# Attention and a two-expert part on one core: the attention's loop over pairs of batches written out batch by batch

## Chip, cores and metric

The kernel runs on one core of a Trainium2 chip. The metric is the device time of one execution in microseconds (us), lower is better; before the change three runs gave 1580.22, 1586.92 and 1582.1 us, median 1582.1.

## The reference

For x of 8 batches x 512 positions x 512 channels, in 32-bit floats:

```
xn  = (x - mean) / sqrt(var + 1e-5)                     # per position
qkv = xn @ Wqkv.T + b_qkv                               # 16 heads of 32
p   = softmax(q k^T / sqrt(32) + slope[h] * (k - 511), causal)
s   = (p v) @ Wout.T + b_out
e   = argmax(softmax(xn @ w_router.T)); w = its weight  # one of 2 experts per position
h   = xn @ w_fc[e].T;   a = (h if h >= 0 else h/2)^2    # 2048 wide
g   = silu(w * (a @ w_proj[e].T))
out = x + s * g
```

## The kernel before, in words

There are two blocks, one after the other, with a barrier between them. `attention_block` computes s for all positions and the routing table (which expert, its weight, the position's rank). `ffn_block` then runs 17 slots of 256 positions each, every slot with one expert's weights; it reads s back by gathered rows and writes the output by scattered rows. Its instructions are all written out, slot by slot (`slots`, a Python loop).

In `attention_block` every engine (TensorE, ScalarE, VectorE, GpSimd and the DMA queue of SyncE) has a function `iteration(b, odd)` that issues its share of "batch b". An iteration has 16 steps, one per head. In each step TensorE transposes the four causal strips of the normalised weights of one head (10 transposes of 128x128, `ptrans`, line 439, 160 in a batch), runs one or two jobs of the list `JOBS` (projections q, k, v, the output projection "o", the transposes of xn "x", the router's "logits" and "rank", and the weighted sum "ctx"), and computes the scores of a head four steps ahead (`scores`, line 418). VectorE masks scores and takes their minimum (line 791), forms reciprocals (line 802), and has the layer norm's statistics of the next batch in steps 0 and 1 (lines 683, 684), its application in steps 2 to 5 (line 690), and in step 13 `place`, a chain of small operations on 128x4 elements (lines 741 to 757), each of which waits for the one before through the semaphore `dve_link` (`link`). ScalarE exponentiates (line 562) and evacuates PSUM. GpSimd multiplies the weights by the reciprocals (line 872), forms the low 16-bit parts of q and k (line 878), and in step 1 takes the layer norm's inverse root (lines 884 and 887). SyncE stores q and k parts to DRAM and loads them again head by head (`stack`, lines 277 and 282).

The order of the work on each engine is the order written out by hand in `JOBS` and `STEP`. Engines agree through counting semaphores: each wait asks for a count that depends on b, such as "(b * H + h) * QB + i + 1".

Which iterations run is set by `batches`, called once by each of the five engines: iterations -1 and 0 are written out, then a hardware loop `Fori` runs three times over a body that holds two iterations (b = 1 and 2, 3 and 4, 5 and 6), then 7 and 8 are written out. Each engine runs its own loop. The odd and even iterations use different halves of the double buffers, which is why the body holds two.

In the loop b is a register's value. What depends on it is then worked out at run time: the count that a wait compares with (register operations, line 86), the DRAM address of a transfer, and for VectorE, GpSimd and SyncE also an increment of a semaphore of its own (`apart`) that belongs to such a wait, so that the wait is an instruction by itself ahead of the one that needs it (line 88). Where b is a number, the wait's count is a constant and most waits stand inside the instruction that needs them:

```
def wait(eng, sem, value, apart=None):
    if isinstance(value, int) and value <= 0:
        return
    eng.wait_ge(sem, value)
    if apart is not None and not isinstance(value, int):
        eng.sem_inc(apart, 1)
```

`within` and `job_exists` decide whether b exists at all; for a register's value they say yes. For b = 1 to 6 all jobs exist, in either form.

Of the kernel before, what the change touches and what calls it, by code (L numbers as in the profile page):

```python
# [25 lines left out]
B, S, D = 8, 512, 512  # L26
# [68 lines left out]

def batches(eng, iteration):

    iteration(-1, 1)
    iteration(0, 0)
    with eng.Fori(0, (B - 2) // 2) as it:  # L100
        iteration(it * 2 + 1, 1)
        iteration(it * 2 + 2, 0)
    iteration(B - 1, 1)
    iteration(B, 0)

WEIGHTS = ["q", "k", "logits", "v", "o"]  # L110
# [25 lines left out]
def attention_block(nc, io, sc, conf, esum, mall, eslot, eint, tint):  # L136

    with ExitStack() as ctx:
# [113 lines left out]
        def _(sp):  # L252
# [33 lines left out]
            def iteration(b, odd):  # L286
# [23 lines left out]
                if within(b, -1, B - 1):  # L310
                    stack(b + 1, 0)
                    stack(b + 1, 1)

            batches(sp, iteration)
            sp.wait_ge(s["meta_out"], 16 * QB * B)
            sp.dma_start(mall[:].rearrange("p t (h c) -> p (t h) c", c=MROW),
# [6 lines left out]
        def _(pe):  # L323
# [158 lines left out]
            pe.sem_inc(s["O_done"], 1)  # L482
            pe.wait_ge(s["const_in"], 16)
            batches(pe, iteration)

        @block.scalar
        def _(act):
# [42 lines left out]
            def iteration(b, odd):  # L530
                more = within(b, -1, B - 1)
                for step in range(H):
# [43 lines left out]
                    if more and step == 12:  # L576
                        wait(act, s["nd_ready"], b + 2)
                        nc.scalar.activation(ex[:], nd[:], ACT.Exp).then_inc(s["rexp_done"], 1)

            batches(act, iteration)  # L580

        @block.vector
# [707 lines left out]
```

## Time and profile before

| | us |
|---|---|
| median of 3 runs | 1582.1 |
| the profiled execution, its own time | 1582.49 |
| its span (first to last instruction) | 1579.8 |
| TensorE busy | 1426.5 (90%) |
| VectorE busy | 940.1 (60%) |
| ScalarE busy | 774.1 (49%) |
| GpSimd busy | 691.5 (44%) |
| last transpose of a head's weights (line 439) | 782.9 |

The profile is one execution. PE is TensorE's matmuls, PEld its weight loads, DVE VectorE, ACT ScalarE, POOL GpSimd, SP SyncE. A "q" behind an engine's name is its sequencer, which works out registers, branches and issues DMAs; "issue" as the end of an idle time means that the engine waited for nothing that the profile shows. PEclk is TensorE's granted clock as a share of full speed. A row of a window reads: start and end from the span's start, its length, then for PE, PEld, DVE, ACT and POOL the busy time and in brackets the number of instructions, then PEclk, the mean busy share of the 16 DMA engines and the GB/s that they moved. Where times of steps are given, a step begins with the first of its ten transposes.

### The profile page before, as it was taken

The numbers are of one execution on the slowest core, as the hardware profiler recorded it, in microseconds if no ns is written. First come the engines' busy times: TensorE is split into PE (matmuls) and PEld (weight loads), VectorE is DVE, ScalarE is ACT, GpSimd is POOL, SyncE is SP. The second block draws the span as 40 slices with busy tenths as digits, with TensorE's granted clock in tenths as the row PEclk, the third lists the DMA queues.
The fourth block names the chain that finished last, engine by engine and source line by source line (L and its number), as shares of the span: only waits on it lengthen the run. The fifth ranks groups of instructions, "written<-read, shape, count | busy, mean of one in ns | idle before, by whom it ended". The sixth has DMA issues, their size and how long they took to land. (4 is left out here: it accounts for less than half of the span.)

```text
span 1579.8 us, 32881 instructions
## 1 busy us (share of the span) xinstructions
PE 1426.5 (90%) x9912; PEld 902.2 (57%) x9912; DVE 940.1 (60%) x2432; ACT 774.1 (49%) x1826; POOL 691.5 (44%) x900
## 2 busy tenths in 40 slices
PE   2889999979999799999749999999999999999995
PEld 1455555645555355555426666666666666666663
DVE  7567776757667567776628954544444545545442
ACT  3477776757777567777606532222222222222221
POOL 0456556545555556556513443333333333333321
PEclk9999999989999899999969999999999999999998
DMA  4424334232533324333146611110111111111000
GB/s 150 155 86 135 101 116 140 88 116 88 158 98 101 114 87 145 101 114 122 41 131 218 202 41 33 32 32 28 41 41 39 30 41 41 41 41 42 17 21 31
DMA packets 85162, 134.24 MB, mean 85 GB/s; under 512 B 14207, under 2 KB 63359, under 8 KB 82816
## 3 DMA queue, kind: packets, MB, share of 16 engines
q1 hardware_dynamic: 75808, 105.70, 20.9%
q0 software_dynamic: 9184, 26.36, 5.3%
q8 instruction: 96, 1.57, 0.4%
q14 instruction: 74, 0.61, 0.1%
HBM read 98.34 MB, written 34.21 MB: 84 GB/s over the span
## 5 line engine op out<-in xcount | busy, mean ns | idle before, releaser
L1018 PE MATMUL psF<-xT,wf 128*128 128x256 f16 x3264 | 381.8, 274 | 6.7 <-DVE wf L1121 6.7
L1036 PE MATMUL psY<-wf,aT 128*128 x1632 | 374.3, 379 | 0.0
L1018 PEld LDWEIGHTS psF<-xT,wf 128*128 x3264 | 320.9, 98 | 74.2 <-issue 7.4
L1224 POOL TENSOR_TENSOR a<-a 128x512 f32<-128x512 f32 x136 | 156.7, 1152 | 410.3 <-DVE a L1138 408.8
L872 POOL TENSOR_SCALAR pr<-pr,rden 128x128 f32<-128x128 f32 (+3 forms) x512 | 269.5, 545 | 151.0 <-DVE rden L802 149.7
L562 ACT ACTIVATE pr<-pr,mn 128x128 f32<-128x128 f32 (+3 forms) x512 | 281.8, 553 | 0.0
L791 DVE CUSTOM_DVE_ANT_0 pr<-psS,base,nsl 128x128 f32<-128x128 f32 (+3 forms) x512 | 250.4, 544 | 16.9 <-issue 12.4
L1036 PEld LDWEIGHTS psY<-wf,aT 128*128 128x128 f16 x1632 | 159.8, 98 | 163.8 <-issue 0.2
L439 PE MATMUL psT<-conf,pr 128*128 128x128 f32 x1280 | 210.0, 283 | 37.7 <-POOL pr L872 23.7
L439 PEld LDWEIGHTS psT<-conf,pr 128*128 128x128 f32 x1280 | 160.6, 145 | 103.9 <-issue 36.5
L345 PE MATMUL psA<-xT,wqkv 128*128 128x512 f16 x768 | 196.4, 395 | 20.2 <-DVE wqkv L644 13.1
L1072 ACT ACTIVATE rl<-psF 128x512 f32<-128x512 f32 x136 | 81.2, 597 | 267.6 <-PE psF L1018 267.6
L549 ACT ACTIVATE pt<-psT 128x512 f32<-128x512 f32 x256 | 151.7, 593 | 115.0 <-PE psT L439 105.7
L1138 DVE SCALAR_TENSOR_TENSOR a<-psF,rl 128x512 f32<-128x512 f32 x136 | 94.0, 691 | 183.1 <-ACT rl L1072 182.2
L1079 ACT ACTIVATE aT<-a 128x512 f16<-128x512 f32 x136 | 85.7, 630 | 228.5 <-POOL a L1224 228.5
L1145 DVE TENSOR_TENSOR aT<-a,aT 128x512 f16<-128x512 f32 x136 | 93.6, 688 | 128.5 <-ACT aT L1079 118.4
L345 PEld LDWEIGHTS psA<-xT,wqkv 128*128 128x128 f16 x768 | 76.9, 101 | 92.9 <-issue 17.6
L878 POOL TENSOR_TENSOR pre<-stage,pre 128x512 f16<-128x512 f32 x64 | 74.3, 1161 | 124.6 <-DVE pre L716 124.6
L418 PE MATMUL psS<-ks,qs 128*128 128x128 f16 (+3 forms) x512 | 101.5, 304 | 28.3 <-DVE mn L791 23.3
L716 DVE CAST pre<-stage 128x512 f16<-128x512 f32 x64 | 31.3, 489 | 125.4 <-ACT stage L502 125.2
L562 ACT ACTIVATION_READ_ACCUMULATOR pr<-pr,mn 128x1 f32 x512 | 98.3, 192 | 0.0
L345 PE MATMUL psA<-wqkv,xT 128*128 128x512 f16 x384 | 96.6, 395 | 0.4 <-ACT stage L502 0.4
(137 smaller groups left out, 1385.5 us busy)
## 6 DMA issues: line engine op xcount, KB each, us to landing
qk_parts<-pre SPq DMA_DIRECT2D x64, 256.0 KB, 2.2
qs<-qk_parts SPq DMA_DIRECT2D x128, 128.0 KB, 2.6
ks<-qk_parts SPq DMA_DIRECT2D x128, 128.0 KB, 2.6
wst<-in_wf SPq DMA_DIRECT2D x16, 1024.0 KB
wstage<-in_wf SPq DMA_DIRECT2D x32, 512.0 KB, 4.6
xin<-in_x SPq DMA_DIRECT2D x32, 256.0 KB
attn_out<-so SPq DMA_DIRECT2D x32, 256.0 KB, 2.2
pt<-in_wqkv SPq DMA_DIRECT2D x4, 768.0 KB, 10.3
```

The costliest lines, as they stand in the source:

```text
L345: last = nc.tensor.matmul(ps, a, x, start=(n == 0), stop=(n == len(pairs) - 1))
L418: nc.tensor.matmul(rows[i], qs[:, par, j, i * P:(i + 1) * P], ks[:, par, j, 0:(i + 1) * P], start=True, stop=True).then_inc(s["S_done"], 1)
L439: last = nc.tensor.transpose(ps[:, o:o + P], pr[:, j, c:c + P], conf[:, C_ID:C_ID + P])
L549: nc.scalar.activation(pt[:, g % 2, j, o:o + w], psT[r][:, 0:w], ACT.Copy).then_inc(s["T_act"], 1)
L562: nc.scalar.activation(p_, p_, ACT.Exp, bias=mn[:, c:c + 1], scale=-1.0, accum_out=den[:, c:c + 1]).then_inc(s["exp_done"], 1)
L791: nc.vector.tensor_tensor_reduce(out=pr[:, h % HG, ROWOFF[i]:ROWOFF[i] + w], in0=rows[i], in1=base[:, S - w:S], scale=nsl[:, h:h + 1], sca ...
L872: nc.gpsimd.tensor_scalar(p_, p_, rden[:, c:c + 1], 32768.0, ALU.mult, ALU.mult).then_inc(s["norm_done"], 1)
L1018: last = nc.tensor.matmul(psF[c % 2][:, k * TT:(k + 1) * TT], w(e, 2 * hc, hl, kc * 512 + col, P), xT[:, r % 2, x, kc, :], start=(m == 0), ...
L1036: last = nc.tensor.matmul(psY[r % 2][h][:], aT[:, c % 4, x, k, h * P:(h + 1) * P], w(e, 2 * hc + 1, hl, q * 512, 512), start=(c == 0 and k ...
L1138: nc.vector.scalar_tensor_tensor(out=a[:, c % 2, :], in0=psF[c % 2][:], scalar=2.0 ** -28, in1=rl[:, c % 2, :], op0=ALU.mult, op1=ALU.add) ...
L1145: tt(aT[:, c % 4, 1, :, :].rearrange("p k n -> p (k n)"), a[:, c % 2, :], aT[:, c % 4, 0, :, :].rearrange("p k n -> p (k n)"), ALU.subtrac ...
L1224: nc.gpsimd.tensor_tensor(at, at, at, ALU.mult).then_inc(s["a_ready"], 1)
```

## The change

In `batches`, the loop and the four calls around it become a Python loop over b = -1 to 8, which calls `iteration` ten times with a number. Nothing else is edited; all five engines call `batches`. So the bodies of iterations 1 to 6 are written out, on every engine, with constant counts and addresses; the increments of the `apart` semaphores are not issued any more. `ffn_block` does not call `batches`.

```
 def batches(eng, iteration):
 
-    iteration(-1, 1)
-    iteration(0, 0)
-    with eng.Fori(0, (B - 2) // 2) as it:
-        iteration(it * 2 + 1, 1)
-        iteration(it * 2 + 2, 0)
-    iteration(B - 1, 1)
-    iteration(B, 0)
+    for b in range(-1, B + 1):
+        iteration(b, b % 2)
```

## Rows read from the trace of the kernel before

**Rows 1.** The page: busy us of each engine, share of the span, instructions.

```profile
PE 1426.5 (90%) x9912; PEld 902.2 (57%) x9912; DVE 940.1 (60%) x2432; ACT 774.1 (49%) x1826; POOL 691.5 (44%) x900
```

**Rows 2.** Windows: iterations 0 to 6, then the rest after the attention's transposes.

```profile
67.20:150.00 82.80, 73.62 (x532) 45.01 (x530) 60.06 (x220) 65.70 (x182) 50.28 (x80) 0.96 0.39 121
150.00:242.10 92.10, 85.97 (x610) 51.02 (x611) 64.83 (x225) 65.84 (x182) 52.92 (x82) 0.96 0.39 122
242.10:338.20 96.10, 86.21 (x611) 50.80 (x610) 65.68 (x227) 67.01 (x184) 55.81 (x85) 0.96 0.36 117
338.20:433.60 95.40, 86.85 (x611) 51.07 (x612) 64.24 (x225) 65.64 (x180) 49.87 (x80) 0.95 0.34 107
433.60:530.60 97.00, 86.02 (x612) 50.79 (x610) 66.67 (x233) 66.95 (x184) 56.85 (x87) 0.96 0.36 115
530.60:625.70 95.10, 86.94 (x610) 51.09 (x610) 63.30 (x220) 65.71 (x180) 48.80 (x78) 0.95 0.34 103
625.70:714.80 89.10, 82.90 (x610) 49.38 (x610) 64.94 (x226) 66.41 (x182) 52.90 (x82) 1.00 0.35 113
...
783.30:1579.80 796.50, 747.33 (x5113) 501.51 (x5112) 401.99 (x595) 236.19 (x374) 270.79 (x241) 0.97 0.18 57
```

**Rows 3.** Instructions of line 100, the loop: ns min/median/max, first and last start.

```profile
L100 PEldq COMPARE_BRANCH  x3: 83/5699/6773, 332.2 to 714.2; - x3
```

**Rows 4.** Waits, 332 to 342 us (first back edge): engine line <- releaser: us, times, longest.

```profile
DVE rden L802 <- issue: 4.1, 1, 4.1
PE psT L439 <- issue: 3.8, 1, 3.8
...
PE psA L345 <- issue: 2.5, 1, 2.5
```

**Rows 5.** Windows: step 15 and next step 0 of iterations 2/3, 4/5, 6/7.

```profile
328.29:349.76 21.47, 15.18 (x85) 7.68 (x84) 8.14 (x27) 8.09 (x22) 10.55 (x14) 0.76 0.30 104
519.60:541.51 21.91, 15.06 (x85) 7.87 (x85) 8.14 (x27) 8.10 (x22) 10.54 (x14) 0.77 0.32 103
710.25:721.50 11.25, 11.11 (x86) 6.20 (x85) 8.52 (x28) 8.09 (x22) 9.90 (x14) 1.00 0.28 99
```

**Rows 6.** Windows: steps 1 and 2 of iterations 0, 6; step 14 onward of 0, 6.

```profile
71.60:82.65 11.05, 9.07 (x53) 5.24 (x53) 10.22 (x37) 8.98 (x25) 8.24 (x13) 1.00 0.44 141
632.38:644.19 11.81, 9.19 (x57) 5.33 (x53) 9.81 (x35) 8.83 (x23) 8.06 (x13) 1.00 0.43 133
139.05:149.98 10.93, 9.48 (x53) 5.10 (x52) 9.91 (x40) 8.36 (x24) 7.36 (x11) 1.00 0.56 168
702.86:714.83 11.97, 9.48 (x53) 5.10 (x51) 10.08 (x40) 8.20 (x24) 7.36 (x11) 1.00 0.48 150
```

**Rows 7.** Timeline of VectorE: start, us; `place` to next reciprocal, iteration 0.

```profile
139.88 1.03 DVE L745 TENSOR_TENSOR t<-tid,rk 128x4 f32<-128x4 f32 x1
...
142.86 0.17 DVE L802 RECIPROCAL rden<-den 128x4 f32<-128x4 f32 x1
```

**Rows 8.** The same of iteration 6; in brackets the idle time ahead.

```profile
703.69 1.12 DVE L745 TENSOR_TENSOR t<-tid,rk 128x4 f32<-128x4 f32 x1
704.97 0.17 DVE L746 TENSOR_SCALAR t<-tid 128x4 f32<-128x4 f32 x1 [0.16 <-DVE t L745]
...
707.69 0.17 DVE L802 RECIPROCAL rden<-den 128x4 f32<-128x4 f32 x1
```

**Rows 9.** Windows: step 3 of iterations 1, 3; step 15 of iterations 1, 6.

```profile
168.44:174.37 5.93, 5.92 (x27) 3.49 (x28) 1.34 (x6) 3.22 (x9) 4.16 (x6) 0.71 0.15 50
361.56:365.84 4.28, 4.28 (x26) 2.63 (x27) 1.34 (x6) 3.22 (x9) 4.15 (x6) 1.00 0.20 66
236.17:242.13 5.96, 5.96 (x28) 3.46 (x28) 3.76 (x13) 3.22 (x10) 4.14 (x6) 0.71 0.93 269
710.25:714.83 4.58, 4.44 (x27) 2.63 (x26) 4.06 (x13) 3.52 (x10) 4.14 (x6) 1.00 0.48 162
```

**Rows 10.** The page: the queue that loads TensorE's instructions among others.

```profile
q8 instruction: 96, 1.57, 0.4%
```

## The prediction

> **What bounds the kernel now.** I read the page first: TensorE is busy 90% of the span, no other engine above 60% [rows 1]. So the question is what TensorE waits for, and at which clock it works. Next the windows, cut at the first transpose of each iteration [rows 2]. The reader is to see three things. Iterations 1 to 6 hold the same work (610 to 612 matmuls each), yet take 92.1, 96.1, 95.4, 97.0, 95.1 and 89.1 us, 564.8 together. The one at full clock (1.00) is the shortest; the five others stand at 0.95 or 0.96. And in that shortest one TensorE is busy 82.9 of 89.1 us, so idle time is not the large part: it is 6.2 us. Six iterations like the best would take 534.6 us; 30.2 us are lost in the loop against its own best pass, none of it work. The expert part (796.5 us) is not touched, its code is the same, and I let it stand at its own length.
>
> Then I looked for places. I cut the iterations into steps. A given step takes nearly the same time in all six, but for these places: the two changes from iteration 2 to 3 and 4 to 5 (the taken back edges), and steps 3 and 15. A fourth view, the same steps in iteration 0, which is written out already, shows what a loop iteration would look like with constant waits.
>
> **The change part by part.**
>
> A. The two taken back edges go. At the first of them TensorE's branch is recorded with 5699 ns, at the second with 6773, at the third, not taken, with 83 [rows 3]. VectorE's next reciprocal stands 4.1 us idle by "issue" too, TensorE's next transpose 3.8, and then a second time 2.5 us before the projection behind it [rows 4]. An engine that waits for nothing in the profile just behind a jump waits for its own code; TensorE does so twice. After these idle stretches the clock is down. All of it together: step 15 and the next step 0 take 21.47 and 21.91 us with the edge, with a mean clock of 0.76 and 0.77, and 11.25 us where the same two steps follow one another in written-out code, iteration 6 to 7, at 1.00 [rows 5]. That is 10.22 + 10.66 = 20.9 us. It lies wholly on the path, since TensorE is the bound and all engines stall at once. The entry to the loop and its exit show nothing comparable and I cost them at nothing. In the 20.9 are two half-clock stretches of step 15 that come before the edge (1.4 us each, see C); those could return, so A is between 18.1 and 20.9.
>
> The Trainium skill, Advanced Engine Details and Errata, section Control Flow Timing, gives about 108 ns for a compare-and-branch. By it the loop would be nearly free, A would be 0.2 us and the sum 20 us smaller. The trace's 83 ns for the branch not taken fits; the 5699 and 6773 ns of the taken ones do not, and the measurement decides. The page speaks of the branch, not of the code behind it.
>
> B. Waits with a register's count become constants. Each costs a register operation and, on VectorE, GpSimd and SyncE, a wait of its own ahead of the instruction. On most of the 89 us this lies beside matmuls. It does not in two places, where VectorE's or GpSimd's chain releases TensorE. The first is `place` in step 13, whose linked operations are short: in iteration 0 it is 139.88 to 142.86 from its first subtraction to the next reciprocal, 2.98 us [rows 7]; in iteration 6 it is 4.00 us, with an idle 0.15 to 0.16 ahead of each linked one [rows 8]. GpSimd's scaling of the next head follows that reciprocal and TensorE's transposes follow GpSimd. It shows in TensorE's steps: steps 14 and 15 take 10.93 us in iteration 0 and 11.97 in 6, with the same matmul time of 9.48 in both [rows 6]: 1.04 us. The second is the layer norm's statistics in step 1, which GpSimd waits for before its root and before it may scale the next head. Steps 1 and 2 together take 11.05 us in iteration 0 and 11.81 in iteration 6 [rows 6]: 0.76. Iteration 0 lacks the copy of the last context in step 2, but that stands behind the statistics and not on this chain, so I take the difference as it is. B = 1.80 us an iteration, six times: 10.8. Below: nothing, if these differences came from something else in iteration 0. Above: TensorE's whole idle time of iteration 6 outside these places. It is 6.2 less 2.62 (11.81 - 9.19) and 2.49 (11.97 - 9.48), that is 1.1 us, six times 6.6 us more. I take 10.8, the row for row difference.
>
> C. The half clock. In iterations 1, 2, 4 and 5 step 3 is long (5.93 us at a mean clock of 0.71, against 4.28 at 1.00 where it does not fall), and so is step 15 of iterations 1, 2, 3 and 4 (5.96 at 0.71, against 4.58 at 1.00) [rows 9], where one of each kind stands. The matmuls are the same in number; they run at 1.2 GHz instead of 2.4 for a part of the step. One costs 1.65 us in step 3 and 1.4 in step 15. Without the two that A holds there are six: 4 x 1.65 + 2 x 1.4 = 9.4, by the windows 30.2 - 20.9 = 9.3, so the account of the loop closes. What did TensorE before each fall? In step 2 and in step 14, just ahead, it stands idle for most of the 2.62 and 2.49 us above. It fell in 8 of those 12 occasions. In iteration 0 the same steps have 11.05 - 9.07 = 1.98 and 10.93 - 9.48 = 1.45 us of idle, and the clock is 1.00 through both windows and stays there in the step behind [rows 6]: 0 of 2. B brings iterations 1 to 6 to those values. From both sides: none of the eight returns, or all eight (11.9 us). I take the nearer row, iteration 0, but with one of the eight kept, 1.65 us, since two occasions are few and 1.98 is not far from 2.62. So C gives 9.3 - 1.65 = 7.65.
>
> D. What is added: four more iteration bodies of code on each engine. Their instructions are issued in any case, so what counts is whether code arrives in time when read straight on. Iteration 0 is read straight on, and its TensorE works through 532 matmuls with no stall of the back edge's kind; so is the whole expert part, where TensorE is busy 747.33 of 796.5 us [rows 2]. I cost it at nothing. DMAs are the same in number, on the same queue; SyncE merely issues them without register work, so they come no later. When iterations take 87 us, the q and k parts have less time for their way through DRAM, but iteration 0 has them in time in 82.8 us [rows 2].
>
> **The sum.** 20.9 + 10.8 + 7.65 = 39.3 us. Against the profiled execution, 1582.49 us: 1543.2. That execution lies 0.4 us above the median of the runs shown (1582.1), which spread over 6.7 us; I give 1543.
>
> **Rivals.**
>
> 1. The clock falls as before: A and B come, but all eight half-clock stretches return. For it: it fell after two thirds of such idle times, and when a fall comes depends on more than the idle time, as the four spared occasions show. Against: iteration 0. Time: 1582.5 - 18.1 - 10.8 = 1553.6.
>
> 2. Only the edges count; the waits were hidden, and the difference of iteration 0 is due to the output jobs it lacks. The clock then falls as before too. Time: 1582.5 - 18.1 = 1564.4. Against: step 14 has the same 9.48 us of matmuls in both, and the idle gaps between VectorE's linked operations are seen [rows 8].
>
> 3. Slower: straight code comes late. TensorE's code is brought in pieces, 96 of them on the queue of [rows 10] over the 1580 us, so about 5.8 in 95 us and 35 in six iterations. If each stopped TensorE for 2.5 us as the second stall behind the edge did [rows 4], it would add 35 x 2.5 = 87 us, and the time would be 1582.5 - 39.3 + 87 = 1630. It decides from 16 such stalls on. Against: the written-out iteration 0 and the expert part show none, and the loop body, read through, shows them behind the jump alone. The Trainium skill, Runtime: NRT & Kernel Launch, section Instruction fetch mechanics, calls the crossing into the next piece mostly hidden, and a taken branch out of the pieces at hand a stall; the trace agrees with the second by its 3.8 and 2.5 us.
>
> 4. The change does less than it says on one engine: it cannot, since all five call the same function; I give it no chance of its own.
>
> **Chances.** The forecast 0.78; rival 1 0.13; rival 2 0.05; rival 3 0.03; another 0.01 near no change. The range goes from the forecast's lower bound, 1543.2 - 1.65 - 6.6 = 1535 with all of B's upper bound, which I cut to 1537 as that end asks every other idle time to go, to beyond rival 1: 1557, a few us for the expert part's own start. A measurement of this kernel tells a difference from no change at about 0.5%, 8 us. Faster 0.96, same 0.01, slower 0.03.
>
> **What would show it.** A: no branch in line 100, and no idle time by "issue" over 2 us between 150 and 680 us on TensorE or VectorE; iterations of equal length, near 87.5 us. B: steps 1 and 2 together near 11.05 and 14 and 15 together near 10.95 in every iteration; the gaps between the linked operations of `place` under 0.05 us. C: granted clock 1.00 in iterations 1 to 6 but for about one stretch. D: the last transpose near 744 us instead of 782.9, the expert part as long as before within 3 us. It is wrong if iterations stay above 89 us, if the clock stands at 0.96 in most, or if TensorE shows idle times by "issue" that come once in some 15 us.

## The result, and the profile after

The changed kernel takes 1543.35 us (median of 4 runs, 1540.84 to 1544.06) against 1583.9 us before (4 runs). The ratio is 0.9742, 95% interval 0.9716 to 0.9768. The profiled execution has a span of 1542.0 us where before had 1579.8, that is 37.8 us less.

The windows of the changed kernel come first, cut at the first transpose of iterations 1 to 7, and then the part behind the attention's transposes. Columns are those of [rows 2].

```profile
150.80:239.31 88.51, 84.35 (x611) 50.06 (x611) 64.00 (x226) 66.47 (x182) 52.82 (x82) 0.98 0.38 119
239.31:326.07 86.76, 82.70 (x610) 49.26 (x610) 64.50 (x226) 66.45 (x182) 52.82 (x82) 1.00 0.38 122
326.07:414.51 88.44, 84.35 (x610) 50.07 (x611) 64.57 (x226) 66.48 (x182) 52.81 (x82) 0.98 0.38 121
414.51:502.96 88.45, 84.36 (x610) 50.05 (x610) 64.50 (x226) 66.45 (x182) 52.76 (x82) 0.98 0.38 121
502.96:591.41 88.45, 84.35 (x610) 50.07 (x611) 64.50 (x226) 66.48 (x182) 52.80 (x82) 0.98 0.38 120
591.41:679.86 88.45, 84.35 (x611) 50.06 (x611) 64.60 (x226) 66.47 (x182) 52.82 (x82) 0.98 0.36 117
748.20:1542.00 793.80, 744.44 (x5112) 500.42 (x5112) 402.04 (x595) 236.33 (x374) 272.07 (x241) 0.97 0.18 57
```

The six iterations are now almost equal: 529.1 us together against 564.8 [rows 2], 35.7 us less. That is nearly the whole gain. One of them, iteration 2, has the full clock (1.00) and 86.76 us; the five others have a mean clock of 0.98 and 88.4 to 88.5 us. The expert part is 2.7 us shorter (793.80 against 796.50), and the stretches before iteration 1 and from iteration 7 to 748.2 us are together 0.6 us longer.

Next the steps of the changed kernel. The first two rows are steps 1 and 2 (taken as one window) of iterations 1 and 2, the next two steps 14 and 15 of the same iterations, the last two step 3 of iterations 2 and 3.

```profile
157.47:168.68 11.21, 9.02 (x56) 5.38 (x53) 8.99 (x34) 8.83 (x23) 7.92 (x13) 1.00 0.43 133
245.97:257.14 11.17, 9.02 (x56) 5.37 (x53) 9.51 (x35) 8.84 (x23) 7.91 (x13) 1.00 0.43 135
228.47:239.31 10.84, 9.48 (x54) 5.11 (x52) 9.82 (x40) 8.27 (x24) 7.34 (x11) 1.00 0.63 177
315.24:326.07 10.83, 9.48 (x53) 5.10 (x51) 9.80 (x40) 8.27 (x24) 7.34 (x11) 1.00 0.59 170
257.14:261.42 4.28, 4.28 (x26) 2.63 (x27) 1.42 (x6) 3.22 (x9) 4.22 (x6) 1.00 0.25 78
343.90:349.86 5.96, 5.96 (x26) 3.49 (x27) 1.42 (x6) 3.22 (x9) 4.22 (x6) 0.71 0.18 58
```

The reader is to see that steps 1 and 2 went from 11.81 to 11.17 us and steps 14 and 15 from 11.97 to 10.83 [rows 6], and that step 3 still comes in two lengths, 4.28 at full clock and 5.96 at 0.71, as in [rows 9]. Of the six step 3, five are long (4.28 only in iteration 2). Of the six step 15, none is; before, four were.

The timeline of VectorE of the changed kernel, `place` to the next reciprocal in iteration 2:

```profile
316.07 1.02 DVE L737 TENSOR_TENSOR t<-tid,rk 128x4 f32<-128x4 f32 x1
317.13 0.17 DVE L738 TENSOR_SCALAR t<-tid 128x4 f32<-128x4 f32 x1
...
319.05 0.17 DVE L794 RECIPROCAL rden<-den 128x4 f32<-128x4 f32 x1
```

It is 2.98 us, what iteration 0 had [rows 7], not the 4.00 of the loop, and no idle time stands in brackets, as it did in [rows 8]. The loop's line is gone, and no idle time by "issue" of over 1 us is left on TensorE or VectorE in iterations 1 to 6.

### The profile page after: what moved, and what is told of

It reads as the page before. It is cut to its first block and busy times, and to the rows that moved or that the text cites. A ratio compares the mean times of both kernels' runs of the same rounds, so it can differ in the third digit from the quotient of the medians.

```text
span 1542.0 us, 30070 instructions
## 1 busy us (share of the span) xinstructions
PE 1416.1 (92%) x9912; PEld 897.1 (58%) x9912; DVE 936.1 (61%) x2432; ACT 775.3 (50%) x1826; POOL 692.2 (45%) x900
## 5 line engine op out<-in xcount | busy, mean ns | idle before, releaser
L337 PEld LDWEIGHTS psA<-xT,wqkv 128*128 128x128 f16 x768 | 76.9, 101 | 87.5 <-DVE wqkv L636 15.3
L337 PE MATMUL psA<-wout,cx 128*128 128x512 f16 x384 | 91.2, 379 | 2.7 <-POOL cx L884 2.7
```

Source lines behind the costliest of these rows:

```text
L337: last = nc.tensor.matmul(ps, a, x, start=(n == 0), stop=(n == len(pairs) - 1))
```

## The experiments

All times are medians; "before" was run again on the same chip beside each group (1583.13, 1583.65 and 1583.98 us), and ratios are to it.

**TensorE without the loop, the others with it.**

```
 def batches(eng, iteration):
+    if eng.engine.name in ("SP", "Activation", "DVE", "Pool"):
+        iteration(-1, 1)
+        iteration(0, 0)
+        with eng.Fori(0, (B - 2) // 2) as it:
+            iteration(it * 2 + 1, 1)
+            iteration(it * 2 + 2, 0)
+        iteration(B - 1, 1)
+        iteration(B, 0)
+        return
     for b in range(-1, B + 1):
         iteration(b, b % 2)
```

> TensorE's iterations are written out, the other four engines keep the hardware loop of before. Theory (each engine pays for its own jump, and TensorE is late only as far as the others are): TensorE's branch of 5.7 and 6.8 us is gone, but VectorE and ScalarE still stand 3.4 to 4.1 us at each of the two edges, and TensorE waits for them in the step after. Part A falls from 20.9 us to between 6 and 12; the register waits of VectorE and GpSimd stay, so part B is not gained. Time 1568 to 1575. Rival 1 (TensorE's jump alone is the loss): A is gained in full and the time is 1560 to 1564. Rival 2 (any engine's stall stops all alike): no gain, 1580 to 1584.

Measured: 1567.27 us, ratio 0.989 (0.9862 to 0.9918). Below are the windows of step 15 and the next step 0 at the two edges, and then the waits around the first edge.

```profile
324.45:340.35 15.90, 13.04 (x86) 6.42 (x85) 9.58 (x33) 7.86 (x22) 11.09 (x16) 0.89 0.48 151
509.44:527.70 18.26, 14.71 (x86) 7.28 (x85) 10.20 (x37) 7.87 (x22) 11.95 (x18) 0.81 0.43 135
```

```profile
DVE rden L803 <- issue: 4.6, 1, 4.6
ACT pt L550 <- issue: 4.1, 1, 4.1
```

These two steps take 11.3 us without an edge, in this kernel as in [rows 5]. So the jumps of the others alone cost 4.6 and 7.0 us, of the second of which 1.3 are a half-clock stretch in step 15 ahead of the edge; with TensorE's jump too they cost 10.2 and 10.7. At the first edge VectorE and ScalarE stand still for 4.6 and 4.1 us. At the second the profile puts VectorE's 5.2 us down to ScalarE, and ScalarE's idle time by "issue" is weak evidence of a jump: the kernel with register counts and no loop, further below, has four such idle times of 3.2 to 3.6 us. The time lies 0.7 us below the range that the theory gave, nearly on it.

**The loop on TensorE alone.** The same edit with `("PE",)` for the names.

> TensorE alone keeps the hardware loop; VectorE, ScalarE, GpSimd and SyncE are written out. Theory: the waits of VectorE and GpSimd become short, so an iteration at full clock takes 86.8 us (2.3 less than before, 14 us in six), while TensorE still stands 3.8 and 2.5 us at each taken edge and then runs at half clock for a while: about 18 us stay. Time 1561 to 1566. Rival (part B comes from TensorE's own register operations): iterations stay at 89.1 us and the time is 1575 to 1584.

Measured: 1568.63 us, ratio 0.9907 (0.9884 to 0.993), 2.6 us above the theory's range and far from the rival's. Its branch of line 101 and the same windows at the edges:

```profile
L101 PEldq COMPARE_BRANCH  x3: 83/5711/7777, 327.3 to 700.2; - x3
```

```profile
323.76:347.06 23.30, 14.18 (x85) 7.33 (x85) 8.35 (x27) 8.09 (x22) 10.54 (x14) 0.78 0.32 104
512.29:532.28 19.99, 13.31 (x85) 7.11 (x85) 8.34 (x27) 8.09 (x22) 10.54 (x14) 0.83 0.35 120
```

TensorE's jump alone costs 12.0 and 8.7 us, as much as all five jumps together. The price of the jumps does not add up over the engines: 4.6 and 7.0 for the others, 12.0 and 8.7 for TensorE, 10.2 and 10.7 for all. The branches of the engines lie within 4 us of each other in the kernel before (SyncE's apart), so they stand still at about the same time.

Whether an engine waits for its own code behind its jump, the two queues of kind "instruction" can say something about (packets, MB, busy share). Below are 10 us around the first edge: of the kernel before (332 to 342), of the loop on TensorE alone (327 to 337), and of the loop on the four others (328 to 338).

```profile
q8 instruction: 3, 0.05, 1.9%
q14 instruction: 4, 0.03, 1.1%
```

```profile
q8 instruction: 2, 0.03, 1.2%
q14 instruction: 1, 0.01, 0.3%
```

```profile
q8 instruction: 1, 0.02, 0.6%
q14 instruction: 4, 0.03, 0.9%
```

In the changed kernel packets of q8 come 9 to 26 us apart through iterations 1 to 6. TensorE's jump is followed by extra packets of q8, the others' jumps by extra packets of q14. That these are the code at the jump's target is inferred from when they come.

**One-pass loops.**

```
-    for b in range(-1, B + 1):
-        iteration(b, b % 2)
+    iteration(-1, 1)
+    iteration(0, 0)
+    for n in range((B - 2) // 2):
+        with eng.Fori(n, n + 1) as it:
+            iteration(it * 2 + 1, 1)
+            iteration(it * 2 + 2, 0)
+    iteration(B - 1, 1)
+    iteration(B, 0)
```

> All engines: three hardware loops of one pass each in place of one of three passes, so that no backward branch is taken and the code is read straight on, while b stays a register's value. It separates A from B. Theory: A is gained, 18 to 21 us, B is not: steps 1 and 2 together take 11.8 us and steps 14 and 15 12.0 (both at full clock), an iteration 89.1 us plus the half-clock stretches, which come behind step 2 and step 14 as before. Time 1561 to 1570. Rival 1 (the register waits are hidden and the gain was all in the edges): 1543 to 1547. Rival 2 (straight reading has a price of its own, which the constant waits paid for): over 1575.

Measured: 1545.25 us, ratio 0.9756 (0.9732 to 0.9781). This seems to speak for rival 1, but it does not, since the experiment missed its aim. The counts came out as constants, as a loop of one pass has one value of its index: the trace has no register operation on line 86 any more, where before had 552 on VectorE and 480 on ScalarE. What it shows is small, but useful. Below are its iterations 1 to 6 in one window and its part behind the last transpose, and then that part of the changed kernel.

```profile
150.95:680.01 529.06, 504.42 (x3661) 299.62 (x3661) 386.48 (x1351) 398.75 (x1087) 317.52 (x492) 0.98 0.38 120
748.19:1545.67 797.48, 747.68 (x5114) 501.21 (x5113) 401.93 (x595) 236.84 (x374) 274.00 (x241) 0.97 0.18 57
```

```profile
747.75:1541.97 794.22, 744.86 (x5114) 500.44 (x5113) 402.04 (x595) 236.75 (x374) 272.07 (x241) 0.97 0.18 57
```

A loop's own instructions with the branch not taken cost nothing: the six iterations take 529.1 us as in the changed kernel, and five of six step 3 are long in both. And the part behind them, which no edit touches, differs by 3.3 us between the two executions.

**No loop, register counts.** For iterations 1 to 6, b is a register on four engines; SyncE keeps the constants.

```
+    zero = 0
+    if eng.engine.name in ('PE', 'Activation', 'DVE', 'Pool'):
+        eng.wait_ge(ZERO[1], 1)
+        zero = eng.value_load(ZERO[0][0:1, 0:1], min_val=0, max_val=1)
+    for b in range(1, B - 1):
+        iteration(zero + b, b % 2)
```

> No loop at all, all iterations written out, but for iterations 1 to 6 the number b on TensorE, ScalarE, VectorE and GpSimd is a register (a zero read from a tile, plus a constant), so that every wait's count is worked out at run time again and the separate waits with their increments are back. SyncE keeps constants. It separates B from A, which the one-pass loops could not do, since the counts became constants there. Theory: an iteration at full clock takes 89.1 us instead of 86.8, so 14 us come back, and with the longer idle time of step 14 the half clock of step 15 can return (up to 6 x 1.4). Time 1557 to 1566. Rival (the register work is hidden, and what iterations gained came with the loop's removal): 1541 to 1547.

Measured: 1569.36 us, ratio 0.9906 (0.987 to 0.9943). The register operations are back, and then the windows of the six iterations, first, second and last, and their sum:

```profile
L86 DVEq ALU_OP  x544: 40/40/57, 148.6 to 697.8; - x182
L86 ACTq ALU_OP  x476: 35/35/38, 148.9 to 700.8; - x159
```

```profile
148.20:240.62 92.42, 85.94 (x611) 51.10 (x612) 64.88 (x226) 65.89 (x182) 52.91 (x82) 0.96 0.39 125
240.62:332.59 91.97, 85.87 (x611) 50.90 (x610) 65.39 (x226) 66.24 (x183) 52.91 (x82) 0.96 0.36 116
...
609.39:701.33 91.94, 85.80 (x611) 50.93 (x610) 65.24 (x226) 66.24 (x183) 52.90 (x82) 0.96 0.33 104
sum 553.13, PE 515.49 PEld 305.72 DVE 391.46 ACT 397.12 POOL 317.44; mean PE 85.91 PEld 50.95 DVE 65.24 ACT 66.19 POOL 52.91
```

Steps 1 and 2 take 11.8 us and step 14 7.4 again, as expected. More came back than the theory's range held, 26.0 us, 3.4 above its upper end: in this kernel the clock falls to half in all twelve occasions, step 3 and step 15 of each of six iterations. So in these profiled executions the constants are worth 553.1 - 529.1 = 24.0 us in the six iterations, and the removal of the loop (with SyncE's register counts) 564.8 - 553.1 = 11.7; by the medians the second is 14.3 (1583.65 - 1569.36). Both shares hold the clock's falls, whose number differs from trace to trace.

**Register counts on VectorE alone.** As the last one, on `("DVE",)`.

> As the run with register counts, but on VectorE alone. Theory: VectorE's linked chains hold most of B: steps 14 and 15 together take 11.9 us instead of 10.8 and steps 1 and 2 0.2 to 0.3 more, 1.3 to 1.6 us an iteration, 8 to 10 in six; the half clock of step 15 can return as well. Time 1551 to 1560. Rival (the share of VectorE is small, TensorE's or GpSimd's own register work matters): under 1547.

Measured: 1559.21 us, ratio 0.9837 (0.9804 to 0.9869), in the theory's range. Its second iteration has no half clock in it and takes 88.1 us, 1.4 more than 86.8: step 14 is 7.2 us instead of 6.2, and steps 2 and 6 are each a quarter of a microsecond longer. Three of its step 15 are long, where the changed kernel has none. Of the 2.3 us of an iteration VectorE's chains hold 1.4. TensorE's own register counts cost another 0.5: in the kernel with the loop on TensorE alone, which has register counts there too, steps 2, 4, 6 and 14 take 26.04 us together at full clock, in the changed kernel 25.51. The remaining 0.4 was not told apart.

**The idle time of step 2 filled.** The changed kernel with

```
                     g, j = step // HG, step % HG
+                    if step == 3 and within(b, 0, B):
+                        ps = bank(b, STEP[3][0])
+                        for _ in range(8):
+                            nc.tensor.matmul(ps[:], wqkv[:, 0, 0, 0:P], xT[:, odd, 0, 0, :],
+                                             start=True, stop=True)
                     ptrans(b, g, j, 0)
```

> The kernel after the change, and in iterations 0 to 7 TensorE runs 8 matmuls of 128x512 more, whose results are never used, in the idle time at the end of step 2, before the transposes of step 3 (1.7 us of work at full clock in 1.8 us of idle). Theory (the half clock of step 3 answers to the idle time of step 2): the clock stays full in step 3 of iterations 1 to 6, step 3 takes 4.28 us in all six instead of 5.96 in five of them, and 5 x 1.68 = 8.4 us are gained: 1533 to 1538. Rival (the clock falls for something else, such as the total of the work, or the extra work delays the transposes): no gain, 1542 to 1548.

Measured: 1537.31 us, ratio 0.9713 (0.9687 to 0.9739). The windows of iterations 1, 2 and 6, and the sum of the six:

```profile
149.89:236.72 86.83, 84.46 (x619) 49.97 (x619) 64.54 (x226) 66.45 (x182) 52.99 (x82) 1.00 0.39 123
236.72:323.51 86.79, 84.45 (x618) 49.96 (x619) 64.51 (x226) 66.47 (x182) 52.92 (x82) 1.00 0.39 123
...
583.87:670.66 86.79, 84.46 (x619) 49.97 (x619) 64.60 (x226) 66.47 (x182) 52.93 (x82) 1.00 0.37 119
sum 520.77, PE 506.74 PEld 299.86 DVE 387.23 ACT 398.77 POOL 317.62; mean PE 84.46 PEld 49.98 DVE 64.54 ACT 66.46 POOL 52.94
```

Eight more matmuls in each iteration, and each is faster or as fast: the clock is 1.00 in all six, all six step 3 take 4.3 us, and 529.1 - 520.8 = 8.3 us are gained, as the theory has it. The median gains 6.0. The difference is not the doing of the matmuls: the part behind the last transpose, which they don't touch, takes 797.1 us in this trace, near the 797.5 of the one-pass kernel, and 794.2 in the changed kernel's. The half clock of step 3 answers to the idle time ahead of it. But that idle time does not decide alone: with 2.5 to 2.7 us of it in steps 1 and 2 the clock fell in step 3 in four of six iterations of the kernel before and of the one with TensorE written out, and in six of six with register counts and no loop. What decides between them was not tried.

**The root behind the scaling.**

```
-                        elif step < 6:
-                            ln_apply(step - 2)
+                        elif (0 if b >= 0 else -1) <= step - 3 < (4 if b >= 0 else 3):
+                            ln_apply(step - (3 if b >= 0 else 2))
...
+                    if more and step == (2 if b >= 0 else 1):
+                        (veps and rstd, as they were)
                     for kind, bj, i, _, _ in jobs(b, odd, step, ("q", "k")):
...
-                    if more and step == 1:
-                        (veps and rstd)
```

> The kernel after the change, and for iterations 0 to 6 GpSimd takes the layer norm's inverse root in step 2 behind the scaling of the next head instead of in step 1 ahead of it; VectorE applies the layer norm in steps 3 to 6 instead of 2 to 5. Theory: TensorE's 1.8 us of idle time ahead of step 3 is GpSimd's root (1.4 us) standing before the scaling; it goes, and with it the half clock of step 3. That is 1.5 to 1.8 us in seven iterations and 1.68 in five: 19 to 21 us, less what the later layer norm costs ahead of the transposes of xn. Time 1522 to 1532. Rival 1 (the later layer norm makes TensorE wait in steps 5 or 6 for as long): 1535 to 1545. Rival 2 (the idle time only moves to another step and the clock falls there): 1538 to 1548.

Measured: 1539.74 us, ratio 0.9734 (0.97 to 0.9767). The time lies in the ranges of both rivals, and the steps decide for rival 2: steps 5 and 6 are together 0.2 us longer, not 1.5 or more. The windows of iterations 2 and 4:

```profile
233.48:320.41 86.93, 82.54 (x611) 49.30 (x611) 63.82 (x226) 66.58 (x182) 52.79 (x82) 1.00 0.39 124
407.33:495.93 88.60, 84.22 (x610) 50.02 (x610) 63.82 (x226) 66.58 (x182) 52.78 (x82) 0.98 0.38 119
```

At full clock an iteration takes 86.93 us, no less than 86.76. Step 2 fell from 6.89 to 4.91 us, and step 3 rose from 4.28 to 6.34; the half clock then fell in step 4, in three iterations. My theory that the root's place costs TensorE its idle time is wrong. GpSimd's timeline in iteration 2 shows why: from the scaling of step 2 to that of the next head it has no gap.

```profile
247.22 2.06 POOL L864 TENSOR_SCALAR pr<-pr,rden 128x128 f32<-128x128 f32 x4 [0.87 <-DVE rden L794]
249.37 0.24 POOL L870 TENSOR_SCALAR veps<-mv 128x4 f32<-128x4 f32 x1
249.70 1.04 POOL L873 TENSOR_TENSOR rstd<-veps,half 128x4 f32<-128x4 f32 x1
250.73 1.15 POOL L879 TENSOR_TENSOR pre<-stage,pre 128x512 f16<-128x512 f32 x1
251.85 1.15 POOL L884 TENSOR_TENSOR cx<-cf,cx 128x512 f16<-128x512 f32 x1
253.09 2.54 POOL L864 TENSOR_SCALAR pr<-pr,rden 128x128 f32<-128x128 f32 x4
```

**Less on GpSimd.** The kernel with the root behind the scaling, and in it the low part of a batch's last context is formed by VectorE instead of GpSimd (VectorE's lines come first, then GpSimd's).

```
+                            if not g:
+                                wait(dve, s["ctx_hi"], pb * NG + pg + 1)
+                                nc.vector.tensor_tensor(cx[:, pg, 1, :], cf[:], cx[:, pg, 0, :], ALU.subtract
+                                                        ).then_inc(s["ctx_lo"], 1)
...
-                    if j == (3 if g else 2) and within(pb, 0, B):
+                    if g and j == 3 and within(pb, 0, B):
```

> The kernel of e5_root_behind_scaling, and the low part of the last context of a batch (step 2) is formed by VectorE instead of GpSimd. In e5's trace GpSimd works without a gap from the scaling of step 2 through the root, the low part of q and of the context (1.15 us) to the scaling of the next head, and TensorE stands idle 1.90 us ahead of step 4. Theory (GpSimd's own load bounds these steps, not the place of the root): the idle time falls to 0.7 to 0.8 us, the clock stays full behind it, an iteration takes 85.7 to 86.0 us, and the time is 1525 to 1532. Rival (VectorE is late instead, by its 0.69 us more ahead of its reciprocal): 1535 to 1542.

Measured: 1525.36 us (1524.54 to 1525.94), ratio 0.9626 (0.9607 to 0.9646). The windows of iterations 2 and 3, and TensorE ahead of step 4:

```profile
231.95:317.36 85.41, 82.52 (x611) 49.28 (x611) 65.27 (x227) 66.60 (x182) 51.28 (x81) 1.00 0.40 124
317.36:402.76 85.40, 82.53 (x610) 49.29 (x610) 64.70 (x227) 66.56 (x182) 51.25 (x81) 1.00 0.38 123
```

```profile
252.64 0.66 PE L431 MATMUL psT<-conf,pr 128*128 128x128 f32 x4 [0.40 <-POOL pr L868]
```

The idle time fell from 1.90 to 0.40 us, further than the 0.7 to 0.8 expected. All six iterations take 85.4 us at full clock, 0.3 less than the theory's lower end, and the time lies in its range. This version beats both kernels, the changed one by 18 us. It was GpSimd's load in these steps that bounded TensorE.

## Why the prediction was right, and where its terms were off

The forecast was 1543 us, the median is 1543.35. The mechanisms of A and B are right; that the number is met to half a microsecond is luck, as the sum is better than its terms. By the medians the gain is 40.6 us (1583.9 - 1543.35), by the spans 37.8, against 39.3 forecast.

A, the edges, was right in its place and as a difference of windows: steps 15 and 0 went from 21.47 and 21.91 us to 11.3 each, 20.7 against 20.9. That the jumps cost this time is shown by the two mixed kernels, for TensorE's jump alone and for the four others together; for each of the four by itself it is not. That the engines wait there for their own code fits the packets of q8 and q14. What the loop's removal is worth by itself was not 18.1 to 20.9: with the register counts kept, the six iterations gain 11.7 us (14.3 by the medians), since the clock, which before fell in 8 of 12 occasions, then falls in 12. Whether the jumps had spared the four is not shown: with register counts on VectorE alone, and no jump, the clock falls in 7 of 12. "A is between 18.1 and 20.9" held only in company with B.

B, the constant counts, was undersized. I gave 1.80 us an iteration; an iteration at full clock went from 89.10 to 86.76, 2.34 us, 14.0 in six instead of 10.8. The two places were right: 0.64 (forecast 0.76) and 1.14 (1.04). The rest, 0.56 us, lies in steps 4 and 6, for which iteration 0 had no counterpart, as it lacks the output jobs, and which I had held in the upper bound of 1.1. The mechanism is shown: register counts put back 24.0 us, falls of the clock included, and 1.4 us an iteration at full clock on VectorE alone.

C, the half clock, is the step that was mis-sized. I forecast that one of the eight stretches stays; five stayed, all in step 3, at 1.68 us each. In step 14, where the idle time fell from 2.49 to 1.35 us (10.83 - 9.48), no fall is left, as forecast. In steps 1 and 2 it fell from 2.62 to 2.15 us (11.17 - 9.02), and there the clock fell in five of six, not less often than before. Iteration 0's "0 of 2" mixed a place that was cured with one that was not. Its step 3 was no accident: it is at full clock in all ten traces, in the changed kernel behind 2.1 us of idle time in steps 1 and 2, as much as the 2.15 behind which iterations 1 to 6 fall. Iteration 0, which does less work, was no sample for the others there, and the idle time was not the whole cause that I took it for. (By C's own terms all eight stretches are 12.2 us, not the 11.9 written there; nothing in the sum rests on it.) Outside the windows of A I had 7.65 us for C and 0.9 came (9.3 - 5 x 1.68). That the fall follows the idle time is shown by the filled kernel, in which the work grows and all falls are gone.

Together: 20.7 + 14.0 + 0.9 = 35.6 us in the iterations against 39.3 forecast, and the windows give 35.7. The expert part gave 2.7 us that I had put at nothing, rightly as far as the change goes. From the last transpose to the end the ten traces take 794.2 to 798.1 us, with no edit that touches this part; the changed kernel's is the shortest, and the one-pass kernel, equal to it in the iterations, has 797.5. Some 3 us of the scatter lie ahead of the first expert matmul (41.9 to 45.0 us behind the last transpose); what makes it is open. So B's excess of 3.2 us, which has a cause, and the expert part's 2.7, which lie within that part's scatter, stand against C's loss of 6.8.

D, the added code, was right at nothing: no idle time by "issue" that comes once in some 15 us is in the trace, though packets of q8 come that often, and rival 3 is out. Of the signs that I named, C's failed (five stretches, not one), the last transpose came at 747.7 us and not near 744, and five iterations took 88.4 to 88.5 us, not 87.5. Rival 1, all falls return, was right for step 3, where more came (five) than before (four), and its time of 1553.6 was wrong by the size of B and by step 15. Rival 2, the waits are hidden, is refuted by the runs with register counts.

## What to carry to other kernels

Price a hardware loop from its own trace: compare the steps at the back edge with the same steps where code is written out, and compare the counts' cost on the engine whose short dependent chain releases the bounding one. When a change shortens idle time on a TensorE-bound path, take the clock's stretches as terms of their own, place by place, and do not carry a sample from one place to another. A match of the total proves little where unlike terms can cancel: compare part by part, and compare the part that the change does not touch over several traces to learn its scatter. If idle time stays after a rearrangement, look at whether the releasing engine has any gap left at all: if not, take work off it rather than reorder it.

## What the runs showed of the hardware

The branch's price is split differently in the records: TensorE's own record holds it (5699, 6773, 5711 and 7777 ns in four jumps), the other engines' branches are recorded with 40 to 68 ns and the stall stands behind them, 4.1 and 3.4 us on VectorE at the two edges of the kernel before. On GpSimd the root of a 128x4 tile took 1.04 us, almost as long as a subtraction of 128x512 (1.15 us); few elements made it no cheap operation. And eight more matmuls of 128x512 in an iteration made the kernel 6 us faster.
